# Value and output weights of a local attention folded into one matrix per head, in a six-layer stack on one core

## The chip, the cores and the metric

The program runs on one core of one Trainium2 chip. The metric is the device time of one execution in microseconds (us), the median of several runs.

## What is computed

The input x has 8 batches of 512 tokens with 128 features. Two blocks follow each other, each behind a layer norm that is scaled and shifted per batch, and each is added to x with a gate. The first block is a causal attention with 16 heads of 8. The second is a stack of 6 layers; each is a windowed attention with 16 heads of 64 followed by a gated feed-forward part, both on x with its upper 64 features shifted by one token:

```python
def attn_layer(x, Wqkv, qs, ksc, Wo):
    q, k, v = jnp.split(x @ Wqkv, 3, -1)          # each 1024 wide: 16 heads of 64
    q = l2norm(q) * qs; k = l2norm(k) * ksc       # then rotary tables on both
    out = local_attention(q, k, v)                # windows of 32, each sees itself and the one before
    return out.reshape(b, n, INNER) @ Wo          # 1024 -> 128

for i in range(6):
    x = attn_layer(shift_tokens(x), Wqkv[i], q_scale[i], k_scale[i], Wo[i]) + x
    x = ffn_layer(shift_tokens(x), ln_g[i], ln_b[i], W1[i], b1[i], W2[i], b2[i]) + x
```

All of it is float32. A head's part of the result is softmax(q k) times v_h times Wo_h, where v_h = x Wv_h is 64 wide and Wo_h takes 64 to 128.

## The kernel before

There are three stages, one after the other: `modulated_attention` (names `at_`), `local_stack` (names `st_`), and a short `last_residual` (`lr_`). Every engine has its own hand-written program, with loops that are unrolled by hand at both ends, and semaphores between the engines.

**The first attention** goes through the batches, with 16 steps to a batch, one head a step. Its TensorE order is a table, `M_JOBS`: (step, part, kind, batch offset, index). These products go in turn into two PSUM banks, and each waits until the one two places before has been taken out. Beside them, in batches 1 to 6, this stage prepares one layer of the stack per batch: the SP queue loads a third of Wqkv (`split_weights`, the q, k or v part, 128x1024), GpSimd splits it at L1516 and L1518 into a rounded part and a remainder (two fp32r numbers in place of one float32), and SP stores both in a DRAM scratch, `wqkv_parts`. The rotary tables are made in the same batches.

**The stack** has 6 layers times 8 batches, so 48 units, and a unit is four steps, one for each tile of 128 tokens: 192 steps in all. A step works on four tiles at once, in a software pipeline. For the new tile it makes q, k and v (L455): for each, 6 fp32r products of 128x512, three per half of the width. For the tile one back it transposes the rotated q and k (`tq`, `tk`, L472) and multiplies them (`sim`, L485: for each of 8 head pairs and 4 windows a product that has 32 output rows). For the tile two back it transposes the weights (`pt`, L477) and multiplies them with v (`o`, L497: again 8 times 4 products with 32 output rows). For the tile three back it transposes o (`ot`, L505) and multiplies with Wo (`z`, L465), which gives the layer's result with features on the partitions. Once a unit come the products of the feed-forward part of earlier units: `m1` in step 3, `m2` in step 0, `h` in step 1 and `y` in step 2. The order of TensorE is the list in `jobs_of`; `slot_free` makes each product wait until the last user of its PSUM banks has been read out.

The others, for each step:

- VectorE sums the squares of q (L710), multiplies it with the cosines (L714) and the sines (L728, two halves), then the same for k; L721 puts a floor under the sums. Then come mask (L749), maximum (L753), the sum of the weights and its reciprocal (L757, L760), the addition of z to x (L784), and the division of o by the sums (L792).
- GpSimd adds the cosine and sine parts of q and of k (L826 twice), makes one Newton step for the norms (four small operations, L833 to L839), multiplies q and k with them (L846 twice), and subtracts the maximum from the scores of the tile one back (L874). In step 1 it does five operations of the feed-forward norm first (L853 to L861).
- ScalarE squares q and k, copies the transposed tiles out of PSUM, copies v to `v_tok`, and takes the exponentials.
- The SP queue builds `v_bd`, the values of each window with those of the window before, by ten DMAs a step from `v_tok` (`spread_v`, L371 to L379; eight in step 0): 64 partitions x 2 KB each for three of four windows, 32 partitions for the rest. It waits for the `o` product that still reads the half of `v_bd` it writes.

At the last unit of a layer SP loads the next layer's `wqkv` (three DMAs of 1 MB, L337), as soon as the last tile's q, k and v have been made.

## Time and profile before

| | |
|---|---|
| time, median of 3 runs | 3995.38 us (3992.62 to 4001.01) |
| the profiled execution: its own time | 4002.27 us |
| its span, first to last instruction | 4000.5 us |
| mean granted TensorE clock in it | 0.985 of full speed |
| TensorE busy (PE) | 3733.8 us, 93% |
| its weight loads (PEld) | 2927.6 us, 73% |
| VectorE busy (DVE) | 3151.4 us, 79% |
| ScalarE busy (ACT) | 2570.7 us, 64% |
| GpSimd busy (POOL) | 2781.7 us, 70% |

Busy is the time in which at least one instruction of an engine runs. PE and PEld run beside each other. A row of a list of groups gives the source line, the engine, the operation, what is written and what is read, the number of instructions, and then the busy time and the mean of one; matmuls overlap in the array, so their mean is longer than the busy time divided by their number. A row of a timeline has the start in us from the beginning of the span, the length in us, the instruction, and how many were merged. DMA share is how busy the 16 DMA engines were on average.

### The profile page before, as it was taken

What the parts mean: (1) busy time and instruction counts of PE and PEld (TensorE: products, weight loads), DVE (VectorE), ACT (ScalarE), POOL (GpSimd) and SP (SyncE); (2) the same over time, 40 slices, a digit from 0 to 9 for tenths busy, and PEclk for the clock granted to TensorE, in tenths of its full rate; (3) what the DMA queues carried; (4) which work ended last, traced back from release to release, by engine and by line L of the source; (5) the groups of instructions that cost most, each with busy time, mean ns of one, the idle gap of its engine ahead of it and who ended that gap; (6) DMA issues with size and microseconds to landing.
All of it is one profiled execution on the core that took longest, in us unless ns stands there. A gap on an engine that the chain in (4) does not pass through costs nothing. (4 is left out here: it accounts for less than half of the span.)

```text
span 4000.5 us, 109740 instructions
## 1 busy us (share of the span) xinstructions
PE 3733.8 (93%) x42284; PEld 2927.6 (73%) x42284; DVE 3151.4 (79%) x4328; ACT 2570.7 (64%) x3589; POOL 2781.7 (70%) x2249
## 2 busy tenths in 40 slices
PE   6998897799999999999999999999999999999996
PEld 4766675677777777777777777777777777777774
DVE  4666664888888888888888888888888888888884
ACT  3555554566666666666666666666666767676763
POOL 2554552777777777777777777777777777777772
PEclk9999998999999999999999999999999999999998
DMA  1122110322223222232222232222322223222222
GB/s 42 59 74 73 66 68 13 100 66 60 62 63 100 66 58 64 55 103 63 68 53 66 82 79 64 61 61 62 102 66 62 60 60 99 62 70 54 68 54 62
DMA packets 157178, 267.01 MB, mean 67 GB/s; under 512 B 32062, under 2 KB 51644, under 8 KB 152380
## 3 DMA queue, kind: packets, MB, share of 16 engines
q1 hardware_dynamic: 157116, 266.19, 24.7%
q8 instruction: 38, 0.62, 0.1%
q14 instruction: 24, 0.20, 0.0%
HBM read 44.81 MB, written 26.21 MB: 18 GB/s over the span
## 5 line engine op out<-in xcount | busy, mean ns | idle before, releaser
L826 POOL TENSOR_TENSOR st_qk_rot<-st_qk_rot,st_qk_sq 128x1024 f32<-128x1024 f32 x384 | 920.5, 2402 | 692.7 <-DVE st_qk_sq L728 692.7
L455 PE MATMUL st_ps<-st_wqkv,st_xs 128*128 128x512 f32 x3456 | 949.6, 410 | 25.8 <-issue 18.3
L455 PEld LDWEIGHTS st_ps<-st_wqkv,st_xs 128*128 128x128 f32 x3456 | 608.2, 189 | 194.6 <-issue 75.2
L846 POOL TENSOR_TENSOR st_qk_rot<-st_qk_rot,st_rn 128x1024 f32<-128x1024 f32 x384 | 723.1, 1904 | 15.0
L710 DVE TENSOR_REDUCE st_nt<-st_qk_sq 128x16 f32<-128x1024 f32 x384 | 466.2, 1214 | 234.6 <-ACT st_qk_sq L573 233.2
L728 DVE TENSOR_TENSOR st_qk_sq<-st_ps,st_rot 128x512 f32<-128x512 f32 x768 | 490.1, 678 | 0.0
L714 DVE TENSOR_TENSOR st_qk_rot<-st_ps,st_rot 128x1024 f32<-128x1024 f32 x384 | 466.1, 1214 | 9.8 <-PE st_ps L472 9.8
L472 PE MATMUL st_ps<-consts_sb,st_qk_rot 128*128 128x128 f32 x3072 | 402.2, 274 | 27.9 <-DVE st_hid L802 14.9
L571 ACT ACTIVATE st_qk_sq<-st_ps 128x512 f32<-128x512 f32 x192 | 115.0, 599 | 486.3 <-PE st_ps L455 485.8
L472 PEld LDWEIGHTS st_ps<-consts_sb,st_qk_rot 128*128 128x128 f32 x3072 | 355.8, 141 | 94.1 <-DVE st_hid L802 34.7
L465 PEld LDWEIGHTS st_ps<-st_oT,st_wo 128*128 128x128 f32 x3072 | 368.8, 192 | 69.5 <-issue 67.7
L1458 DVE TENSOR_REDUCE at_nmx<-at_s 128x1 f32<-128x512 f32 (+3 forms) x512 | 236.9, 486 | 209.3 <-PE at_s L1103 208.5
L608 ACT ACTIVATE st_k_bd<-st_ps 64x1024 f32<-64x1024 f32 x384 | 389.5, 1014 | 3.1 <-PE st_ps L472 0.8
L485 PE MATMUL st_ps<-st_k_bd,st_qT 128*32 128x128 f32 x12288 | 375.2, 274 | 3.0 <-ACT st_k_bd L608 3.0
L465 PE MATMUL st_ps<-st_oT,st_wo 128*128 128x128 f32 x3072 | 376.2, 276 | 0.5 <-ACT st_oT L632 0.3
L497 PE MATMUL st_ps<-st_v_bd,st_probT 128*32 128x128 f32 x12288 | 375.2, 274 | 1.3 <-ACT st_probT L640 1.3
L874 POOL TENSOR_TENSOR st_s<-st_s,st_mx 128x1024 f32<-128x1024 f32 x192 | 366.0, 1906 | 6.1 <-DVE st_mx L753 6.1
L1279 ACT ACTIVATE at_probT<-at_t 128x512 f32<-128x512 f32 (+1 forms) x384 | 201.3, 526 | 255.8 <-PE at_t L1122 248.1
L485 PEld LDWEIGHTS st_ps<-st_k_bd,st_qT 128*32 128x32 f32 x12288 | 326.4, 110 | 35.6 <-ACT st_k_bd L608 20.5
L497 PEld LDWEIGHTS st_ps<-st_v_bd,st_probT 128*32 128x32 f32 x12288 | 323.7, 110 | 24.5 <-issue 1.5
L522 PE MATMUL st_ps<-st_xc,st_w 128*128 128x512 f32 (+1 forms) x576 | 261.8, 604 | 52.6 <-DVE xT_sb L784 43.2
L1542 POOL TENSOR_TENSOR at_qs<-at_q,consts_sb 128x512 fp32r<-128x512 f32 x128 | 135.3, 1074 | 216.8 <-DVE at_q L1409 200.0
(144 smaller groups left out, 6944.8 us busy)
## 6 DMA issues: line engine op xcount, KB each, us to landing
st_v_bd<-st_v_tok SPq DMA_DIRECT2D x1152, 128.0 KB, 2.4
st_v_bd<-st_v_tok SPq DMA_DIRECT2D x672, 64.0 KB, 2.1
wqkv_parts<-at_w_parts SPq DMA_DIRECT2D x18, 1024.0 KB, 4.6
st_wqkv<-wqkv_parts SPq DMA_DIRECT2D x18, 1024.0 KB, 7.0
at_w_raw<-in_wqkv SPq DMA_DIRECT2D x18, 512.0 KB, 5.1
rotary_tables<-at_rot SPq DMA_DIRECT2D x6, 512.0 KB, 3.4
st_rot<-rotary_tables SPq DMA_DIRECT2D x24, 128.0 KB, 2.4
st_wo<-in_wo SPq DMA_DIRECT2D x6, 512.0 KB, 4.4
```

Source lines behind the costliest of these rows:

```text
L455: last = pe.matmul(out[:, c * 512:(c + 1) * 512], xs[:, x_part, t * P:(t + 1) * P], rhs, start=(n == 0), stop=(n == len(PASSES) - 1))
L465: last = pe.matmul(out[:, 0:P], wo[:, c, :], oT[:, c * P:(c + 1) * P], start=(c == 0), stop=(c == IC - 1))
L472: last = pe.transpose(out[:, c * P:(c + 1) * P], src[:, c * P:(c + 1) * P], ident)
L485: last = pe.matmul(out[g * WIN:(g + 1) * WIN, c * P:(c + 1) * P], qT[:, par, c * P + g * WIN:c * P + (g + 1) * WIN], k_bd[:, c, :, key:key ...
L497: last = pe.matmul(out[g * WIN:(g + 1) * WIN, c * P:(c + 1) * P], probT[:, c * P + g * WIN:c * P + (g + 1) * WIN], v_bd[:, par, g, :, c * ...
L608: last = act.activation(k_bd[rows, :, a, WIN + t1 * P:WIN + (t1 + 1) * P], src[rows, :, :], ACT.Copy)
L710: dve.tensor_reduce(nt[:, 2 + par, heads], qk_sq[:, cols].rearrange("p (h d) -> p h d", d=DH), AX.X, ALU.add).then_inc(ss_sum, 1)
L714: dve.tensor_tensor(qk_rot[:, cols].rearrange("p (h d) -> p h d", d=DH), slot_of("qk"[a], 0, t).rearrange("p (h d) -> p h d", d=DH), rot[: ...
L728: last = dve.tensor_tensor(dst[:, :, g, :], src[:, :, 1 - g, :], sines.unsqueeze(1).to_broadcast([P, HEADS, DH // 2]), ALU.mult)
L826: pool.tensor_tensor(qk_rot[:, cols], qk_rot[:, cols], qk_sq[:, cols], ALU.add).then_inc(rot_done[a], 1)
L846: pool.tensor_tensor(view, view, rn[:, par, heads_of(a)].unsqueeze(2).to_broadcast([P, HEADS, DH]), ALU.mult).then_inc(normed[a], 1)
L874: pool.tensor_tensor(scores, scores, mx[:, tt % 2, :].unsqueeze(2).to_broadcast([P, HEADS, 2 * WIN]), ALU.subtract).then_inc(shifted, 1)
```

## The change

The product of the value weights and the output weights of each head, Wv_h Wo_h (128x128), is computed once a layer in the first attention. In the stack v is then x times that, 128 wide a head and 2048 for all 16 heads, in two halves `v0` and `v1` (even and odd heads). The weights times these values are summed over the head pairs directly in PSUM: the `z` product now has the form of the old `o` product, and its 128x128 result, tokens on the partitions, is copied and transposed once (`zt`). `ot` and the product with `wo` are gone. The division by the sums moves from VectorE after `o` to GpSimd before the weights are transposed (`scaled`), so that `pt` and everything after it work on a tile three back. `v_tok` and `v_win` (formerly `v_bd`) hold twice the bytes. The last 32 rows of a tile's values, which the next tile needs, are first copied by DMA into `v_held`. Several banks, and the order of the work on ScalarE and VectorE in a step, are different.

```diff
-H_BANKS = ((0, 1), (6, 7), (2, 3))
+H_BANKS = ((6, 7), (0, 1), (4, 5))
+PROJ = ("q", "k", "v0", "v1")
...
             return [tile("q", 0, 0, 1), tile("tq", 1, 2, 3), tile("k", 0, 4, 5), tile("tk", 1, 6, 7),
-                    tile("v", 0, 2, 3), tile("ot", 3, 0, 1), tile("sim", 1, 6, 7), tile("pt", 2, 2, 3), *feed,
-                    tile("z", 3, 0), tile("o", 2, 4, 5), *hidden]
+                    tile("v0", 0, 2, 3), tile("pt", 3, 0, 1), tile("sim", 1, 6, 7), tile("v1", 0, 0, 1), tile("z", 3, 2),
+                    *feed, *hidden, tile("zt", 3, 7)]
...
+                    for kind in ("v0", "v1"):
+                        sp.wait_ge(taken[kind], tiles_done(u, 0, t))
+                    if t < TILES - 1:
+                        d, carried = ((-1, 3), (-1, 2), (0, 1))[t]
+                        if alive(u, d):
+                            sp.wait_ge(carry_in[carried % 2], carry_count(u, d, carried))
+                        for a in range(2):
+                            sp.dma_start(v_held[held_rows(t, a), :], v_tok[P - WIN:P, par, a, :]).then_inc(held_in[par], 16)
+                    sp.wait_ge(ready["z"], tiles_done(u, 0, t))
...
-                        if what == "wqkv" and t == TILES - 1:
+                        if what == "wqkv" and t >= TILES - 2:
-                            for kind in "qkv":
-                                sp.wait_ge(ready[kind], tiles_done(u, 0, t))
+                            for kind in (("q", "k"), ("v0", "v1"))[t - (TILES - 2)]:
+                                sp.wait_ge(ready[kind], tiles_done(u, 0, TILES - 1))
                                 load_wqkv(layer + 1, kind)
                         spread_v(u, t)
...
+                            elif kind == "z":
                                 pe.wait_ge(taken["pt"], tiles_done(u, d, index))
-                                pe.wait_ge(vbd_in[par], spread_count(u, d, index))
+                                pe.wait_ge(win_in[par], spread_count(u, d, index))
...
                                 for c in range(IC):
                                     for g in range(WPT):
                                         last = pe.matmul(
-                                            out[g * WIN:(g + 1) * WIN, c * P:(c + 1) * P],
+                                            out[g * WIN:(g + 1) * WIN, 0:P],
                                             probT[:, c * P + g * WIN:c * P + (g + 1) * WIN],
-                                            v_bd[:, par, g, :, c * DH:(c + 1) * DH], start=True, stop=True)
+                                            v_win[:, par, g, c * P:(c + 1) * P], start=(c == 0), stop=(c == IC - 1))
...
+                        def copy_v(a):
+                            act.wait_ge(ready[f"v{a}"], n)
+                            if not (start and n < 3):
+                                act.wait_ge(win_in[t % 2], spread_count(u, d2, t2))
+                                if t2 < TILES - 1:
+                                    act.wait_ge(held_in[t2 % 2], held_count(u, d2, t2))
+                            act.activation(v_tok[:, t % 2, a, :], slot_of(f"v{a}", 0, t), ACT.Copy).then_inc(taken[f"v{a}"], 1)
...
-                            dve.tensor_tensor(
-                                o[:, :].rearrange("p (h d) -> p h d", h=HEADS),
-                                slot_of("o", d2, t2).rearrange("p (h d) -> p h d", h=HEADS),
-                                den[:, t2 % 2, 1, :].unsqueeze(2).to_broadcast([P, HEADS, DH]),
-                                ALU.mult).then_inc(taken["o"], 1)
...
+                        d, tt = divmod(t - 2, TILES)
+                        if alive(u, d):
+                            pool.wait_ge(den_ready, 2 * (n - 2))
+                            weights = s[:, tt % 2, :].rearrange("p (h k) -> p h k", h=HEADS)
+                            pool.tensor_tensor(weights, weights, den[:, tt % 2, 1, :].unsqueeze(2).to_broadcast([P, HEADS, 2 * WIN]),
+                                               ALU.mult).then_inc(scaled, 1)
...
-SPLIT_STEPS = (2, 6, 14)
+SPLIT_STEPS = (5, 11)
...
+                    elif kind == "fold":
+                        rows, half = slice(g // 2 * DH, (g // 2 + 1) * DH), g % 2
+                        pe.wait_ge(taken["vt"], count(b, 0, 2, half))
+                        pe.wait_ge(fold_in, (b - 1) * 16 + 16)
+                        for i in range(TILES):
+                            c = TILES * half + i
+                            last = pe.matmul(out[:, i * P:(i + 1) * P], wvT[rows, c, :], wo_l[rows, c, :],
+                                             start=True, stop=True)
```

In `M_JOBS` of the first attention two jobs `vt` (four transposes of the raw value weights each, steps 2 and 3) and four jobs `fold` (four products each, two in step 7, one each in steps 11 and 14) are added for each layer. ScalarE copies both out of PSUM, and VectorE subtracts to get the remainder of each `fold`. GpSimd splits only the q and k parts now. Four parts of 1 MB a layer are stored and loaded, not three.

TensorE's program in the stack, the last step of the second unit (names: `st_s` weights, `st_wqkv` projection weights, `xT_sb` is x). Before:

```order
L455 MATMUL st_ps<-st_wqkv,st_xs 128x512 x6
L472 MATMUL st_ps<-consts_sb,st_qk_rot 128x128 x8
L455 MATMUL st_ps<-st_wqkv,st_xs 128x512 x6
L472 MATMUL st_ps<-consts_sb,st_qk_rot 128x128 x8
L455 MATMUL st_ps<-st_wqkv,st_xs 128x512 x6
L505 MATMUL st_ps<-consts_sb,st_o 128x128 x8
L485 MATMUL st_ps<-st_k_bd,st_qT 32x128 x32
L477 MATMUL st_ps<-consts_sb,st_s 128x128 x8
L509 MATMUL st_ps<-xT_sb,consts_sb 128x512
L465 MATMUL st_ps<-st_oT,st_wo 128x128 x8
L497 MATMUL st_ps<-st_v_bd,st_probT 32x128 x32
```

The same step in the changed kernel:

```order
L460 MATMUL st_ps<-st_wqkv,st_xs 128x512 x6
L475 MATMUL st_ps<-consts_sb,st_qk_rot 128x128 x8
L460 MATMUL st_ps<-st_wqkv,st_xs 128x512 x6
L475 MATMUL st_ps<-consts_sb,st_qk_rot 128x128 x8
L460 MATMUL st_ps<-st_wqkv,st_xs 128x512 x6
L480 MATMUL st_ps<-consts_sb,st_s 128x128 x8
L488 MATMUL st_ps<-st_k_bd,st_qT 32x128 x32
L460 MATMUL st_ps<-st_wqkv,st_xs 128x512 x6
L500 MATMUL st_ps<-st_v_win,st_probT 32x128 x32
L507 MATMUL st_ps<-xT_sb,consts_sb 128x512
L469 MATMUL st_ps<-consts_sb,st_z_tok 128x128
```

A fourth group of six projections has come in; the eight transposes of o and the eight products with `wo` are gone; one transpose stands at the end, behind the feed-forward product.

GpSimd's program in a step of the stack, in the changed kernel:

```order
L830 TENSOR_TENSOR st_qk_rot<-st_qk_rot,st_qk_sq 128x1024 [waits st_rot_read_q]
L830 TENSOR_TENSOR st_qk_rot<-st_qk_rot,st_qk_sq 128x1024 [waits st_rot_read_k]
L837 TENSOR_TENSOR st_nt<-st_rn 128x32 [waits st_rn_ready]
L839 TENSOR_TENSOR st_nt<-st_nt,st_ss 128x32 [waits st_pool_own]
L841 TENSOR_TENSOR st_nt<-consts_sb,st_nt 128x32 [waits st_pool_own]
L843 TENSOR_TENSOR st_rn<-st_rn,st_nt 128x32 [waits st_pool_own]
L850 TENSOR_TENSOR st_qk_rot<-st_qk_rot,st_rn 128x1024 [waits st_rot_done_q,st_rn_final]
L850 TENSOR_TENSOR st_qk_rot<-st_qk_rot,st_rn 128x1024 [waits st_rot_done_k,st_rn_final]
L878 TENSOR_TENSOR st_s<-st_s,st_den 128x1024 [waits st_den_ready]
L885 TENSOR_TENSOR st_s<-st_s,st_mx 128x1024 [waits st_max_ready]
```

Before, the ninth of these rows (L878) did not exist; the others are the same.

The SP queue at the last unit of a layer, in the changed kernel, from the last but one tile on:

```order
L349 DMA st_wqkv<-wqkv_parts 128x2048 [waits st_q_ready]
L349 DMA st_wqkv<-wqkv_parts 128x2048 [waits st_k_ready]
L382 DMA st_v_held<-st_v_tok 32x1024 [waits st_v0_taken,st_v1_taken,st_carry_in1]
L382 DMA st_v_held<-st_v_tok 32x1024
L389 DMA st_v_win<-st_v_held 32x1024 [waits st_z_ready,st_held_in1]
L389 DMA st_v_win<-st_v_held 32x1024
L394 DMA st_v_win<-st_v_tok 64x1024 x3
L396 DMA st_v_win<-st_v_tok 32x1024
L394 DMA st_v_win<-st_v_tok 64x1024 x3
L396 DMA st_v_win<-st_v_tok 32x1024
L349 DMA st_wqkv<-wqkv_parts 128x2048 [waits st_v0_ready]
L349 DMA st_wqkv<-wqkv_parts 128x2048 [waits st_v1_ready]
```

Before, the three loads of `st_wqkv` stood together, ahead of the last tile's ten DMAs. Now the loads for `v0` and `v1` stand behind ten DMAs that wait for a `z` product. (One load of a rotary table, which stands ahead of the last two rows and another ahead of the first two, is not shown.)

## Rows read from the trace of the kernel before

**Rows 1.** Stretches: PE, PEld, DVE, ACT, POOL busy, clock, DMA share, GB/s
```profile
420.00:500.00 80.00, 71.95 (x533) 54.16 (x533) 52.46 (x108) 46.46 (x90) 44.88 (x40) 1.00 0.20 72
725.00:3948.00 3223.00, 3116.62 (x38250) 2469.24 (x38249) 2699.70 (x3436) 2188.36 (x2860) 2447.53 (x1955) 1.00 0.26 68
```
**Rows 2.** Timeline of TensorE in one step of the stack
```profile
1225.88 1.67 PE L455 MATMUL st_ps<-st_wqkv,st_xs 128*128 128x512 f32 x6
1227.38 1.04 PE L472 MATMUL st_ps<-consts_sb,st_qk_rot 128*128 128x128 f32 x8
...
1232.12 1.06 PE L505 MATMUL st_ps<-consts_sb,st_o 128*128 128x128 f32 x8
1233.11 1.96 PE L485 MATMUL st_ps<-st_k_bd,st_qT 128*32 128x128 f32 x64
...
1237.04 1.95 PE L465 MATMUL st_ps<-st_oT,st_wo 128*128 128x128 f32 x16
1238.92 1.96 PE L497 MATMUL st_ps<-st_v_bd,st_probT 128*32 128x128 f32 x64
1240.80 1.66 PE L455 MATMUL st_ps<-st_wqkv,st_xs 128*128 128x512 f32 x6
```
**Rows 3.** Timeline of TensorE: first projection of step 1, step 2, next step 1
```profile
1509.60 1.66 PE L455 MATMUL st_ps<-st_wqkv,st_xs 128*128 128x512 f32 x6
...
1529.59 1.65 PE L455 MATMUL st_ps<-st_wqkv,st_xs 128*128 128x512 f32 x6
...
1576.82 1.65 PE L455 MATMUL st_ps<-st_wqkv,st_xs 128*128 128x512 f32 x6
```
**Rows 4.** Groups of GpSimd from 800 to 3800 us
```profile
L826 POOL TENSOR_TENSOR st_qk_rot<-st_qk_rot,st_qk_sq 128x1024 f32<-128x1024 f32 x358 | 858.5, 2404 | 641.5 <-DVE st_qk_sq L728 641.5
...
L874 POOL TENSOR_TENSOR st_s<-st_s,st_mx 128x1024 f32<-128x1024 f32 x179 | 341.2, 1906 | 0.0
```
**Rows 5.** Timeline of GpSimd: the feed-forward norm of step 1, then a step 2
```profile
1513.91 1.04 POOL L853 TENSOR_TENSOR st_xc<-st_rstd 128x512 f32<-128x512 f32 x1
...
1517.40 1.29 POOL L859 TENSOR_TENSOR st_xc<-st_xc,st_rstd 128x512 f32<-128x512 f32 x1
...
1520.01 4.69 POOL L826 TENSOR_TENSOR st_qk_rot<-st_qk_rot,st_qk_sq 128x1024 f32<-128x1024 f32 x2
...
1536.68 2.38 POOL L826 TENSOR_TENSOR st_qk_rot<-st_qk_rot,st_qk_sq 128x1024 f32<-128x1024 f32 x1 [5.09 <-DVE st_qk_sq L728]
1540.37 2.48 POOL L826 TENSOR_TENSOR st_qk_rot<-st_qk_rot,st_qk_sq 128x1024 f32<-128x1024 f32 x1 [1.31 <-DVE st_qk_sq L728]
1542.81 0.23 POOL L833 TENSOR_TENSOR st_nt<-st_rn 128x32 f32<-128x32 f32 x1
...
1544.11 3.77 POOL L846 TENSOR_TENSOR st_qk_rot<-st_qk_rot,st_rn 128x1024 f32<-128x1024 f32 x2
```
**Rows 6.** Timeline of VectorE in the same two steps
```profile
1517.65 1.07 DVE L721 TENSOR_SCALAR st_ss<-st_nt 128x32 f32<-128x32 f32 x1
...
1538.78 0.32 DVE L721 TENSOR_SCALAR st_ss<-st_nt 128x32 f32<-128x32 f32 x1
```
**Rows 7.** Timeline of the SP queue at a layer change
```profile
1217.97 1.41 SPq L337 DMA_DIRECT2D st_wqkv<-wqkv_parts  x3
1225.89 1.17 SPq L371 DMA_DIRECT2D st_v_bd<-st_v_tok  x2
...
1231.58 0.59 SPq L379 DMA_DIRECT2D st_v_bd<-st_v_tok  x1
```
**Rows 8.** Stretch in that layer change, columns as in Rows 1
```profile
1225.00:1227.00 2.00, 1.90 (x36) 1.46 (x26) 1.59 (x3) 0.73 (x2) 2.00 (x2) 1.00 1.01 430
```
**Rows 9.** The page: DMA issues, KB each, us from issue to landing
```profile
st_v_bd<-st_v_tok SPq DMA_DIRECT2D x672, 64.0 KB, 2.1
```
**Rows 10.** ScalarE from 800 to 3800 us: copies of v to v_tok
```profile
L618 ACT ACTIVATE st_v_tok<-st_ps 128x1024 f32<-128x1024 f32 x179 | 183.7, 1027 | 4.3
```
**Rows 11.** First attention: products with 32 output rows that add up over key tiles
```profile
L1148 PE MATMUL at_m<-at_probT,at_v_pad 128*32 128x512 f32 x256 | 35.0, 619 | 5.2 <-DVE at_k L1409 4.8 <-ACT at_probT L1279 0.4
```

More of the change, by code:

```diff
@@ L232, in local_stack @@
         nt = sb("nt", [P, 4, 2 * HEADS])
-        v_tok = sb("v_tok", [P, 2, INNER])
-        v_bd = sb("v_bd", [P, 2, WPT, 2, INNER // 2])
+        v_tok = sb("v_tok", [P, 2, 2, INNER])
+        v_win = sb("v_win", [P, 2, WPT, INNER])
+        v_held = sb("v_held", [P, INNER])
         qT = sb("qT", [P, 2, INNER])
@@ L240, in local_stack @@
         probT = sb("probT", [P, INNER])
[L241 to L242 removed]
+        z_tok = sb("z_tok", [P, P])
         xc = sb("xc", [P, N])
@@ L382, in unit @@
+                        sp.dma_start(v_win[a * 2 * WIN + WIN:(a + 1) * 2 * WIN, par, 0, :], v_tok[0:WIN, par, a, :])\
+                          .then_inc(win_in[par], 16)
                 def unit(u, layer=None, what=None):
                     for t in range(TILES):
-                        if what == "wo" and t == 2:
-                            sp.wait_ge(ready["z"], tiles_done(u, -1, TILES - 1))
-                            sp.wait_ge(small_in, 64)
-                            load_wo(layer)
@@ L406, in layer_loads @@
                     u0 = layer * BATCH
-                    unit(u0, layer, None if first else "wo")
+                    unit(u0, layer)
                     unit(u0 + 1, layer, None if first else "w12")
@@ L459, in unit @@
                                         last.then_inc(q_half, 1)
-                            elif kind == "z":
-                                pe.wait_ge(taken["ot"], tiles_done(u, d, index))
-                                pe.wait_ge(wo_in, layer_of(u, d) * 16 + 16)
-                                for c in range(IC):
-                                    last = pe.matmul(out[:, 0:P], wo[:, c, :], oT[:, c * P:(c + 1) * P],
-                                                     start=(c == 0), stop=(c == IC - 1))
+                            elif kind == "zt":
+                                pe.wait_ge(taken["z"], tiles_done(u, d, index))
+                                last = pe.transpose(out[:, 0:P], z_tok[:, :], ident)
                             elif kind in ("tq", "tk"):
@@ L767, in unit @@
                                               ALU.subtract).then_inc(taken["m1"], 1)
+                        if alive(u, d1):
+                            dve.wait_ge(taken["sim"], n - 1)
+                            dve.tensor_reduce(mx[:, t1 % 2, :], scores, AX.X, ALU.max).then_inc(max_ready, 1)
+                        if t == 2 and alive(u, 1):
+                            remainder_half(u, 1, 0)
+                        if t == 1 and alive(u, -2):
+                            gate(2)
+                        d3, t3 = divmod(t - 3, TILES)
+                        if alive(u, d3):
+                            dve.wait_ge(ready["zt"], n - 3)
+                            for rows, first in ((LOW, 0), (HIGH, 1)):
+                                x = columns_of(batch_of(u, d3), t3 * P + first, P, rows)
+                                last = dve.tensor_tensor(x, slot_of("zt", d3, t3)[rows, 0:P], x, ALU.add)
+                            last.then_inc(taken["zt"], 1)
+                        if t == 0 and alive(u, 0) and alive(u, -1):
+                            remainder_half(u, 0, 1)
                         if t == 2 and alive(u, -2):
@@ L1074, in _ @@
             def _(pe):
+                for kind in ("vt", "fold"):
+                    pe.sem_inc(ready[kind], PER[kind])
+                    pe.sem_inc(taken[kind], PER[kind])
+                pe.sem_inc(fold_high, PER["fold"])
                 pe.wait_ge(w_in, 80)
```

262 lines of the change are left out of this document (138 added, 124 removed), and 4 rows, old and new, of the table M_JOBS.

## The prediction

> **What bounds the kernel now.** I read the page's busy times first, where TensorE leads with 93% (the table above). Then the table of stretches: in the stack, from 725 to 3948 us, TensorE is busy 3116.6 of 3223 us (97%), at a granted clock of 1.00, the level of 2.4 GHz, with VectorE at 84%, GpSimd at 76% and the DMA engines at 26%; in the first attention it is 71.95 of 80 us (90%) [rows 1]. So both stages are bound by TensorE's own work, and in the stack hardly anything waits for another engine. The timeline gives the size: a unit of four steps is 1576.82 - 1509.60 = 67.2 us, of which step 1, with the large feed-forward product, takes 20.0 us [rows 3], and a plain step (step 0) 1240.80 - 1225.88 = 14.9 us [rows 2]. What matters next is who has room. GpSimd waited 641.5 us for VectorE before L826 [rows 4], in a stretch of 179 steps: 3.6 us of a step.
>
> **TensorE's work in a step.** The start of one group to the start of the next is what a group costs; all from [rows 2].
> - Gone: eight transposes `ot`, 1233.11 - 1232.12 = 0.99 us; eight products with Wo, 1238.92 - 1237.04 = 1.88 us.
> - Added: six projections, 1227.38 - 1225.88 = 1.50 us; one transpose `zt`, an eighth of 0.99, 0.12 us. `zt` waits for ScalarE's copy of z, but a feed-forward product stands between them in each step (`m1` in the listing above), and it is longer than a 128x128 copy.
> - `o` becomes `z` with the same 32 products, 1240.80 - 1238.92 = 1.88 us: nothing.
>
> Together -1.25 us, times 192 steps: **-240 us**. The time saved is real only as long as nobody else is late.
>
> **GpSimd.** Each step gets one operation more, a 128x1024 product with a broadcast operand, the shape of L874: 1.91 us [rows 4]. Its work in a step was 2 x 2.40 (L826) + 1.30 (the Newton step for the norms, 1544.11 - 1542.81) + 3.77 (L846 twice) + 1.91 = 11.8 us [rows 4, 5], and the feed-forward norm adds 1520.01 - 1513.91 = 6.1 us once a unit [rows 5]: 53 us of 67.2. It becomes 4 x 13.7 + 6.1 = 60.9 us, against TensorE's 67.2 - 5.0 = 62.2. So GpSimd goes to 98% of the new period, and the two drive each other: `tq` needs L846, L826 needs the products that VectorE makes once `tq` has read the old tile. The slack that is left, 1.3 us a unit, is as large as one wait of GpSimd between its two L826, 1.31 us [rows 5]. That wait has a cause: L721, a small operation of VectorE, lies across the first L826. It starts at 1538.78 and ends with it (1536.68 + 2.38 = 1539.06), and only then come k's sines, 1.3 us. At 1517.65 it started 0.25 us after L859 and took 1.07 us, to the end of that one [rows 5, 6]. So VectorE waits in L721 for a running GpSimd operation.
> The Trainium skill (page "SBUF — State Buffer", section "Who interferes with whom") says that `tensor_scalar` on VectorE can take the port pair that it shares with GpSimd, and that whoever comes first holds it for the whole instruction. By that rule the trace agrees, with 1.07 us for a 128x32 operation; taken alone, it would put the upper bound below, +125 us, in place of my +38.
> I choose 0.8 us a unit of lost time, a bit over half of one such wait, as TensorE and GpSimd are late in turns: 48 x 0.8 = **+38 us**. Bounds: 0 (60.9 fits into 62.2), and three such waits in a unit (none in step 1, where the feed-forward norm makes GpSimd late anyhow): 60.9 + 3.9 = 64.8, which is 2.6 us over 62.2, +125 us.
>
> **VectorE and ScalarE.** VectorE loses the 128x1024 division, ScalarE trades the copy of o for one of v1 and a small one of z. VectorE was at 84% and gets lighter [rows 1]: nothing for both. Since `pt` now works three tiles back, the new chain sum, division on GpSimd, transpose has a whole step of time: it costs latency, once.
>
> **The DMAs for the windows.** The same ten DMAs a step carry twice the bytes (2.1 MB), and two more go to `v_held`, for which nobody waits. Issue is one each 0.63 us (1225.89 to 1231.58 for nine) and a small one lands 2.1 us after it [rows 7, 9]: 7.8 us from the first issue to the last landing. Issue does not go with bytes: 1 MB loads are issued in 1.41 us for three [rows 7]. The engines moved 68 GB/s at a share of 0.26 [rows 1], so 262 GB/s at most with 2 KB rows, and 430 with 8 KB rows [rows 8]: 2.1 MB take 4.9 to 8.0 us, so D, the whole, is 7.8 to 10 us. What closes a loop is: z done, D, the copy of v0 to `v_tok` (1.03 us [rows 10]), z again (1.88 us, it uses a bank of v0), 0.3 us of handovers. D + 3.2 is 11.0 to 13.2 us, and the plain step is 14.9 - 1.25 = 13.7. Hidden, but with as little as 0.5 us to spare at the upper end. Taken as nothing.
>
> **Layer changes, five.** Before, the three loads stood ahead of the last tile's ten DMAs and had landed when the next unit began (issued at 1217.97, engines full until 1227 [rows 7, 8]). Now v0 and v1 come behind ten DMAs that wait for the `z` of the last step, which ends some 12.5 us into it (13.7 less `m1` and `zt`): with 6.3 us of issue and a rotary table they are issued at about 19.5, and 1 MB at 430 GB/s with 2.1 us to land makes 24. TensorE wants v0 in the next step at 13.7 + 4.7 = 18.4 (1232.12 - 1225.88 - 1.50 = 4.7 for what stands ahead of v [rows 2]). That is 5.6 us of standing still, of which the slack takes back some: 5 x 5 = **+25 us**. Bounds 0 and 9 us each (both loads): 0 to +45.
>
> **First attention, six layers.** Added for each are eight transposes (0.99) and 16 float32 products of 128 columns (1.88 for eight, so 3.76): 4.75 us of TensorE, in a stage where it is busy 90% [rows 1, 2]. GpSimd loses one split of three, which frees nobody. Six times 4.75, and some waits for the copies of `fold`, as two of these follow each other: **+30 us**. Bounds: 10 (the idle tenth takes most) and 50 (each of the four `fold` jobs makes TensorE wait for two copies, about 0.9 us). The stack's first loads are 4 MB and not 3, at 430 GB/s: **+2 us**.
>
> **Sum.** -240 + 38 + 25 + 30 + 2 = -145. The profiled execution took 4002.3 us, 6.9 above the median of 3995.4, so 3857 for it and **3850 us** as a median. A difference of 0.2%, 8 us, is what can be told from no change here.
>
> **The rivals.**
> 1. *GpSimd sets the pace* (0.19). Each plain step keeps the 1.31 us wait, since GpSimd is now nearly always in L826 when L721 comes: a unit of 64.8 us, -240 + 125 + 57 = -58: 3937 us. For it: both rows of L721, and 98% load. Against it: when GpSimd is late by more than that, L721 meets an earlier operation and the wait is hidden, as at 1520.01, where the two L826 run in 4.69 us without a gap [rows 5]. The page's rule named above leads to this rival.
> 2. *Everything fits* (0.22). GpSimd's slack is enough, the layer loads are not missed, the first attention absorbs half: -240 + 5 + 12 + 2, about 3775 us. For it: TensorE at 97% shows how well this order hides waits [rows 1].
> 3. *The window DMAs close the loop, and it is slower* (0.08). If the ten issues took time with their bytes, 1.26 us each, D would be 1.26 x 9 + 2.1 and something for the queue, 14 us. A plain step would be 17.2 us, a unit 3 x 17.2 + 19 = 70.6: 48 x 3.4 + 57 = +220: 4215 us. It decides from D = 12.5 us on, where a unit is 66.0 and the 57 us of the other terms tip it. Against it: issue times of 64 KB and 1 MB are alike [rows 7].
> 4. *The products that now add up in one place lose their overlap* (0.03). The 32-row products run four at a time, 1.88 us for 32 [rows 2]; `z` now adds eight times into the same columns. Were they to run one by one, this is 5.6 us a step more, nearly 5000 us. Against it: L1148 adds up in the same way, with 32 output rows, at 35.0 / 256 = 0.137 us for 512 columns [rows 11], the rate of the products here (1.88 / 64 = 0.029 for 128).
>
> **Chances.** The forecast 0.46, with its own range of 3815 to 3900; rivals 0.19, 0.22, 0.08, 0.03; 0.02 for no visible change, by several bounds at once. Faster by over 0.2%: 0.87; within: 0.02; slower: 0.11. The range that leaves out the two slow cases and a little at both ends is 3765 to 3945.
>
> **What would show it.** A unit (from one first projection of step 1 to the next) of 62 to 64 us; TensorE at 96% or more of the stack and GpSimd at 95%; waits before L830 down from 641 us to under 150; a wait of TensorE of some 5 us at v0 in the first step of a layer, five times; the first attention longer by 25 to 35 us. It is wrong if ScalarE's copies of v wait for DMAs (D too long), or if TensorE waits for L850 in every step.

## The result, and the profile after

| | before | after |
|---|---|---|
| median of 4 runs each | 3997.92 us | 4049.28 us (4040.14 to 4062.88) |
| ratio, 95% interval | | 1.013 (1.010 to 1.017) |
| the profiled execution, its span | 4002.3, 4000.5 us | 4053.2, 4051.4 us |

The kernel became 1.3% slower; 3.7% faster was forecast. The page of the kernel after, busy times:

```profile
PE 3593.3 (89%) x39260; PEld 2654.6 (66%) x39260; DVE 3040.5 (75%) x4160; ACT 2606.9 (64%) x3817; POOL 3112.2 (77%) x2430
```
TensorE is busy 140 us less, and the program takes 51 us more. The columns of the stretches are those of [rows 1]; the first line is its counterpart, the others lie at the first layer change, where loads from DRAM run beside the window DMAs:

```profile
725.00:3948.00 3223.00, 2920.23 (x34566) 2156.66 (x34566) 2587.58 (x3239) 2193.86 (x3038) 2805.26 (x2143) 0.98 0.65 141
1264.00:1266.00 2.00, 2.00 (x26) 1.28 (x18) 2.00 (x3) 1.63 (x3) 1.01 (x1) 1.00 0.95 389
1266.00:1278.00 12.00, 8.12 (x95) 5.79 (x87) 10.16 (x14) 7.43 (x11) 11.69 (x10) 1.00 1.04 255
1278.00:1290.00 12.00, 3.92 (x14) 3.22 (x14) 1.69 (x3) 0.00 (x0) 2.80 (x2) 0.57 0.75 227
```
TensorE fell from 97% to 91% of the stack: 303 us in which it does nothing, where it was 106. The DMA share rose from 0.26 to 0.65. Who waits, from 900 to 3800 us (total, times, longest), in two parts of the list:

```profile
POOL st_qk_rot L830 <- DVE st_qk_sq L736: 230.4, 215, 3.7
ACT st_v_tok L598 <- DMA st_v_win<-st_v_tok: 229.7, 125, 2.9
...
DVE st_den L766 <- ACT st_s L632: 149.4, 125, 2.6
```
The second line did not exist before: ScalarE stands 1.8 us on average, 125 times, in front of a copy of v, until the window DMAs of the tile that had this half of `v_tok` have landed. The page on the DMA issues (KB each, us from issue to landing) says why; [rows 9] had 2.1:

```profile
st_v_win<-st_v_tok SPq DMA_DIRECT2D x1152, 256.0 KB, 4.6
st_v_win<-st_v_tok SPq DMA_DIRECT2D x384, 128.0 KB, 4.8
...
st_wqkv<-wqkv_parts SPq DMA_DIRECT2D x24, 1024.0 KB, 7.8
```
And the timelines of three engines in one step, first the SP queue:

```profile
1493.44 1.17 SPq L389 DMA_DIRECT2D st_v_win<-st_v_held  x2
1494.65 1.96 SPq L394 DMA_DIRECT2D st_v_win<-st_v_tok  x3
1496.65 1.10 SPq L396 DMA_DIRECT2D st_v_win<-st_v_tok  x1
1497.79 2.82 SPq L394 DMA_DIRECT2D st_v_win<-st_v_tok  x3
1500.66 0.79 SPq L396 DMA_DIRECT2D st_v_win<-st_v_tok  x1
```
```profile
1505.64 1.02 ACT L598 ACTIVATE st_v_tok<-st_ps 128x1024 f32<-128x1024 f32 x1 [2.16 <-DMA st_v_win<-st_v_tok]
```
```profile
1506.79 1.95 PE L500 MATMUL st_ps<-st_v_win,st_probT 128*32 128x128 f32 x64 [0.91 <-ACT st_v_tok L598]
```
The last DMA is issued at 1500.66 and lands 4.9 us later, at 1505.56; ScalarE copies at 1505.64, and TensorE has stood still for 0.91 us when `z` may start. Over all steps from 900 to 3800 us the median from the first issue of these ten to the last landing is 12.1 us; before it was 7.8. While only DMAs between parts of SBUF run, the DMA engines are full at 219 GB/s (columns of [rows 1]):

```profile
1496.00:1505.00 9.00, 8.09 (x102) 6.71 (x101) 7.60 (x10) 6.16 (x8) 8.84 (x7) 1.00 1.03 219
```
The layer change, SP queue and TensorE:

```profile
1274.88 0.99 SPq L396 DMA_DIRECT2D st_v_win<-st_v_tok  x1
1275.92 1.25 SPq L367 DMA_DIRECT2D st_rot<-rotary_tables  x1
1277.21 0.94 SPq L349 DMA_DIRECT2D st_wqkv<-wqkv_parts  x2
```
```profile
1272.56 1.64 PE L460 MATMUL st_ps<-st_wqkv,st_xs 128*128 128x512 f32 x6 [0.79 <-DMA st_wqkv<-wqkv_parts]
...
1286.09 2.90 PE L460 MATMUL st_ps<-st_wqkv,st_xs 128*128 128x512 f32 x6 [11.02 <-DMA st_wqkv<-wqkv_parts]
```
The load of v0 is issued at 1277.21 behind the windows and has landed at 1285.95; the six projections behind the pause take 2.90 us and not 1.64, with the clock at 0.57 in that stretch.

**Where the time went.** I measure units from one `m1` product to the next. Before, each is 67.2 us (at the very start and end 67.3 and 66.4), over layer changes too. After, 41 plain ones take 65.5 to 65.9 (the first 67.5 and the last 65.0), and the five over a layer change 78.4, 75.8, 81.3, 76.5 and 76.3. A batch of the first attention (from one `wo` product to the next) goes from 78.2 to 85.2 us and more. Against the forecast of 3857 for the profiled execution, 196 us are missing:

| term | forecast | measured | lost |
|---|---|---|---|
| 41 plain units | 63.0 us (67.2 - 5.0 + 0.8) | 65.7 | 111 |
| 5 over a layer change | 63.0 + 5 = 68 | 77.7 | 48 |
| first weight load | 696.8 + 30 | 744.5 | 18 |
| from there to the first `m1` | 121.0 + 2 | 127.4 | 4 |
| behind the last whole unit (draining, last stage) | | | 15, the rest |

The third row has scatter of its own. The first attention is the same program in the kernel after and in kernels 1 to 10 below, and its first weight load comes between 736.7 and 749.1 us in these eleven traces, with a mean clock of 0.97 to 0.99 from 200 to 700 us.

### The profile page after: what moved, and what is told of

It is laid out like the page before. It is cut to its first block and busy times, and to the rows that moved or that the text cites. A ratio compares the mean times of both kernels' runs of the same rounds, so it can differ in the third digit from the quotient of the medians.

```text
span 4051.4 us, 104528 instructions
## 1 busy us (share of the span) xinstructions
PE 3593.3 (89%) x39260; PEld 2654.6 (66%) x39260; DVE 3040.5 (75%) x4160; ACT 2606.9 (64%) x3817; POOL 3112.2 (77%) x2430
## 5 line engine op out<-in xcount | busy, mean ns | idle before, releaser
L460 PE MATMUL st_ps<-st_wqkv,st_xs 128*128 128x512 f32 x4608 | 1272.6, 412 | 95.8 <-DMA st_wqkv<-wqkv_parts 52.7
L830 POOL TENSOR_TENSOR st_qk_rot<-st_qk_rot,st_qk_sq 128x1024 f32<-128x1024 f32 x384 | 912.1, 2380 | 276.1 <-DVE st_qk_sq L736 276.0
L460 PEld LDWEIGHTS st_ps<-st_wqkv,st_xs 128*128 128x128 f32 x4608 | 815.0, 190 | 332.7 <-issue 189.6
L850 POOL TENSOR_TENSOR st_qk_rot<-st_qk_rot,st_rn 128x1024 f32<-128x1024 f32 x384 | 739.5, 1947 | 15.0
L598 ACT ACTIVATE st_v_tok<-st_ps 128x1024 f32<-128x1024 f32 x384 | 391.1, 1019 | 269.2 <-DMA st_v_win<-st_v_tok 253.2
L500 PE MATMUL st_ps<-st_v_win,st_probT 128*32 128x128 f32 x12288 | 376.5, 275 | 99.2 <-ACT st_v_tok L598 95.5
L500 PEld LDWEIGHTS st_ps<-st_v_win,st_probT 128*32 128x32 f32 x12288 | 325.3, 110 | 174.3 <-issue 165.7
L878 POOL TENSOR_TENSOR st_s<-st_s,st_den 128x1024 f32<-128x1024 f32 x192 | 366.5, 1909 | 4.4 <-DVE st_den L769 4.4
L766 DVE TENSOR_REDUCE st_den<-st_s 128x16 f32<-128x1024 f32 x192 | 233.3, 1215 | 164.3 <-ACT st_s L632 164.3
L625 ACT ACTIVATE st_probT<-st_ps 128x1024 f32<-128x1024 f32 x192 | 197.0, 1026 | 216.0 <-PE st_ps L480 215.9
```

The source lines that it names most:

```text
L460: last = pe.matmul(out[:, c * 512:(c + 1) * 512], xs[:, x_part, t * P:(t + 1) * P], wqkv[:, PROJ.index(kind), w_part, c * 512:(c + 1) * 51 ...
L500: last = pe.matmul(out[g * WIN:(g + 1) * WIN, 0:P], probT[:, c * P + g * WIN:c * P + (g + 1) * WIN], v_win[:, par, g, c * P:(c + 1) * P], ...
L598: act.activation(v_tok[:, t % 2, a, :], slot_of(f"v{a}", 0, t), ACT.Copy).then_inc(taken[f"v{a}"], 1)
L830: pool.tensor_tensor(qk_rot[:, cols], qk_rot[:, cols], qk_sq[:, cols], ALU.add).then_inc(rot_done[a], 1)
L850: pool.tensor_tensor(view, view, rn[:, par, heads_of(a)].unsqueeze(2).to_broadcast([P, HEADS, DH]), ALU.mult).then_inc(normed[a], 1)
L878: pool.tensor_tensor(weights, weights, den[:, tt % 2, 1, :].unsqueeze(2).to_broadcast([P, HEADS, 2 * WIN]), ALU.mult).then_inc(scaled, 1)
```

## The experiments

Kernel 9 was run five times, each of the other ten once. The kernel before took 3996.3 us beside kernels 1, 2, 3 and 7, 3993.0 beside 4, 5, 6 and 8, and 4000.0 beside the last three. The changed kernel's own four runs lie between 4040 and 4063 us, so a single time that differs by less than some 20 us tells little; the units, which repeat within 0.3 us in a trace, tell more. Theory A was that the window DMAs set the unit through ScalarE's copies; its rival that GpSimd does.

**1. Half the bytes.** Each window DMA moves half of its columns; the others keep zeros, so that half of v never reaches `z`. One of the four kinds of DMA, all cut alike:

```diff
-sp.dma_start(v_win[rows, par, g, :], v_tok[(g - 1) * WIN:(g + 1) * WIN, par, a, :])
+sp.dma_start(v_win[rows, par, g, 0:INNER // 2], v_tok[(g - 1) * WIN:(g + 1) * WIN, par, a, 0:INNER // 2])
```


> The changed kernel, but every DMA from v_tok, to v_held and to v_win moves only the first 512 of its 1024 columns (the values behind the rest stay zero, so the weighted sums leave out half of the head pairs); counts, waits and all other work are the same. Theory A, the window DMAs close the loop (last landing, copy of v0, z): a unit falls from 65.7 us to 62.5 to 63.5, ScalarE's waits for DMA before the copies of v (230 us from 900 to 3800) vanish, and the layer changes shrink by a few us each since the engines are free sooner. Theory B, GpSimd sets the pace: a unit stays at 65 to 66 us. In both the first attention stays at 85 us a batch. Time by A about 3900 us, by B about 4030.

Measured: 4015.2 us. A DMA of 128 KB lands after 2.4 us and ScalarE no longer waits for one, but the units are 65.3, some 67.0; layer changes 70.6 to 72.1. Theory A missed: with its wait gone, another stood almost as high, once a unit before the large feed-forward product (it is explained under 3):

```profile
st_v_win<-st_v_tok SPq DMA_DIRECT2D x1152, 128.0 KB, 2.4
```
```profile
PE st_ps L520 <- ACT st_xc L639: 77.6, 38, 2.1
```

**2. No division on GpSimd.** The product of weights and reciprocal sums is left out (z is then not normalised).

```diff
-pool.wait_ge(den_ready, 2 * (n - 2))
-pool.tensor_tensor(weights, weights, den[:, tt % 2, 1, :].unsqueeze(2).to_broadcast(...), ALU.mult).then_inc(scaled, 1)
-pe.wait_ge(scaled, tiles_done(u, d, index))
+pe.wait_ge(exp_ready, tiles_done(u, d, index))
```


> The changed kernel without GpSimd's product of the weights with the reciprocal sums (so the weights are not divided); pt waits for the exponentials instead. Theory A (DMAs close the loop): GpSimd had slack, a unit stays within 0.5 us of 65.7 us and the time at 4030 to 4050 us. Theory B (GpSimd sets the pace): 4 x 1.9 us less work, a unit falls to 62.5 to 63.5 us and the time to about 3920 us.

Measured: 4045.3 us, units 65.7. GpSimd has 1.91 us a step less to do and simply waits longer:

```profile
POOL st_qk_rot L830 <- DVE st_qk_sq L736: 481.0, 260, 3.6
ACT st_v_tok L598 <- DMA st_v_win<-st_v_tok: 225.9, 124, 2.4
```
So GpSimd alone isn't the limit either.

**3. A semaphore for each half of `v_tok`.** v0's copy waits for the four window DMAs that read v0, not for all eight that read `v_tok`.

```diff
-.then_inc(win_in[par], 16)
+.then_inc(win_in[par][a], 16)
...
-act.wait_ge(win_in[t % 2], spread_count(u, d2, t2))
+act.wait_ge(win_in[t % 2][a], spread_count(u, d2, t2))
```


> The changed kernel with one semaphore for each half of v_tok: the copy of v0 waits only for the DMAs that read v0's half, the copy of v1 for those of v1's. Same work, same bytes. Theory A (the copy of v0 waits for the last landing of all ten DMAs): the first half has landed some 3 us earlier, a unit falls from 65.7 us to 63 to 63.5, and ScalarE's DMA waits fall from 230 us to under 40; time about 3930 us. Theory B (GpSimd sets the pace): a unit stays at 65 to 66 us, the wait only changes its name.

Measured: 4047.2 us, units 65.3 and some 67.0, and no wait of ScalarE for a DMA. What had been behind it shows in GpSimd, ScalarE and TensorE of step 1:

```profile
1498.11 1.91 POOL L886 TENSOR_TENSOR st_s<-st_s,st_mx 128x1024 f32<-128x1024 f32 x1
...
1504.81 1.26 POOL L866 TENSOR_TENSOR st_xc<-st_xc 128x512 f32<-128x512 f32 x1
```
```profile
1506.28 0.81 ACT L640 ACTIVATE st_xc<-st_xc,st_ln_b,st_ln_g 128x512 f32<-128x512 f32 x1 [3.04 <-POOL st_xc L866]
```
```profile
1507.39 1.98 PE L521 MATMUL st_ps<-st_xc,st_w 128*128 128x512 f32 x4 [2.02 <-ACT st_xc L640]
```
GpSimd does the feed-forward norm behind the division and the subtraction of the maxima; it ends at 1506.1, so the large product waits 2 us. In the units of 67.0 the clock also falls after that pause (0.74 and 0.84 in the two stretches of 4 us from 1572), and the product takes 7.1 us and not 5.4. Each of the eleven units of 67.0 has one stretch of 3.4 us at the lower level, and none of those of 65.3 has one.

**4. Both together.** Experiments 2 and 3 in one.

> Both walls taken away at once: one semaphore for each half of v_tok, and GpSimd's product of the weights with the reciprocal sums left out. Alone, each left the unit at 65.3 to 67.0 and at 65.7 us. Theory C (two limits of nearly the same height: the window DMAs, and GpSimd, whose late feed-forward norm holds up the large product h): the unit falls to 62.3 to 63.5 us and the wait of TensorE for ScalarE's st_xc (2.0 us a unit) is gone; time about 3920 us. Rival D (some other wait, of TensorE for VectorE or of the order of the products): the unit stays above 64.5 us.

Measured: 3938.4 us, units of 63.2 throughout. Alone, kernel 2 came out 4 us and kernel 3 2 us below 4049, both within the scatter, with units of 65.7 and of 65.3 and 67.0; together they give 111. Two limits of almost the same height: that is theory C, and it holds.

**5. The feed-forward norm first.** Kernel 3, and GpSimd's norm at the end of step 0, ahead of the maxima, with ScalarE's use of it ahead of the exponentials.

```diff
-if t == 1 and alive(u, -2):
+if t == 0 and alive(u, -2):
...
-act.activation(s[:, t2 % 2, :], s[:, t2 % 2, :], ACT.Exp).then_inc(exp_ready, 1)
...
 act.activation(xc[:, :], xc[:, :], ACT.Identity, bias=column(ln_b, P, layer_of(u, -2)),
                scale=column(ln_g, P, layer_of(u, -2))).then_inc(ff_xn, 1)
+act.activation(s[:, t2 % 2, :], s[:, t2 % 2, :], ACT.Exp).then_inc(exp_ready, 1)
```


> One semaphore for each half of v_tok, as before; and GpSimd does the five operations of the feed-forward norm at the end of step 0, ahead of its subtraction of the maximum, not at the start of step 1; ScalarE applies the norm's gain (st_xc) before its exponentials in step 1. Same work, GpSimd's division kept. Theory C: h no longer waits for st_xc (2.0 us), the clock does not fall after that gap, and the unit is 63 to 63.8 us in place of 65.3 and 67.0; time about 3960 us. Rival E (GpSimd's total work is the limit, wherever the norm stands): the unit stays at 65 us or more.

Measured: 3996.3 us (before, on that chip, 3993.0), units 64.6, between the two readings: less gained than expected. Nothing is left out here, and 53 us are back.

**6. Window DMAs in turns over the partition halves.**

```diff
-for a in range(2):
-    for g in range(1, WPT):
+for g in range(1, WPT):
+    for a in range(2):
...
+for a in range(2):
```
(The last loop is now around the two smaller DMAs.)


> The changed kernel with the eight window DMAs of a step issued in turn for partitions 0 to 63 and 64 to 127, instead of four for the one half and then four for the other. Theory P (a transfer over 64 partitions reaches only a part of what the DMA engines can do, so that turns help): landing of the 256 KB ones falls from 4.6 to under 3.5 us, ScalarE's DMA waits from 230 us to under 80. Rival (SBUF to SBUF costs what it costs by bytes): landings and waits stay within 10% and the unit at 65.7 us.

Measured: 4021.5 us, units 65.3. The landings stay at 4.8 and 4.6 us, so that part missed; ScalarE's wait for DMAs fell from 230 to 150 us all the same. The landings of each burst show a path: the last of the ten lands 4.1 us after its issue and no longer 5.1 (medians), and from the first issue to the last landing it is 11.5 us, not 12.1.

**7. All weight loads ahead of the windows.** The four loads of the next layer stand ahead of the last-but-one tile's windows.

```diff
-if what == "wqkv" and t >= TILES - 2:
+if what == "wqkv" and t == TILES - 2:
-for kind in (("q", "k"), ("v0", "v1"))[t - (TILES - 2)]:
+for kind in PROJ:
```


> The changed kernel with all four loads of the next layer's projection weights ahead of the tenth-last tile's DMAs, that is before the window DMAs of the last but one tile's step, as near as possible to where they stood before the change. Theory: the 12 us that each of five layer changes costs over a plain unit (an interval of 75.8 to 81.4 us against 65.7) come from v0's load standing behind ten DMAs. They should fall to 4 us or less each, and the clock should not drop there: 40 to 50 us less, about 4003 us. Rival: the DMA engines are full anyway, 2 MB more ahead of the windows only delays these, and the interval stays above 73 us.

Measured: 4035.8 us, layer changes 73.3 to 75.4, above the 70 expected. The stall moved; its longest is now ScalarE's:

```profile
ACT st_v_tok L598 <- DMA st_v_win<-st_v_tok: 273.1, 129, 10.2
```
Four megabytes ahead of the windows make the windows late.

**8. Loads in the middle.** Kernel 3, with q, k and v0 ahead of those windows and v1 between their halves.

```diff
+next_weights("q", "k", "v0")
+spread_v(u, t, (lambda: next_weights("v1")) if changes else None)
```


> One semaphore for each half of v_tok, as before; and at a layer change the loads for q, k and v0 stand ahead of the last but one tile's window DMAs, v1's load between its two halves. Theory: v0's weights are there when asked for, and the copy of v0 waits for only half of the windows: a layer change costs at most 5 us over a unit (10 to 12 before, 9 with all four loads ahead), so the intervals are 70 to 72 us. Rival: 4 MB of loads and 2.1 MB of windows in one step fill the engines whatever the order, and it stays at 74 us.

Measured: 4022.6 us, layer changes 68.3, 69.9, 73.1, 68.9 and 68.3: 3 to 8 us over a unit, where they were 10 to 16.

**9. The cures together** (3, 5 and 8), timed against before.

> The three cures together: a semaphore for each half of v_tok, GpSimd's feed-forward norm at the end of step 0, and the next layer's weights for q, k and v0 loaded ahead of the last-but-one tile's window DMAs with v1 between its halves. The parts measured 64.6 us a unit (half waits and norm first) and layer changes 3 to 5 us longer than a unit (loads in the middle). If they add: units 64.6, the five intervals over a layer change 67 to 71 instead of 74.6 to 77.3, 30 to 40 us below the run with norm first (3996), so 3955 to 3970, about 1% faster than before. If the loads' traffic meets the earlier norm in a new wait: units stay 64.6 but layer changes 72 or more, 3980 or more.

Measured: 3965.1 us (3962.9 to 3974.6, 5 runs), before 4000.0; ratio 0.992 (0.990 to 0.993). The parts add up as expected: units 64.6; layer changes 70.0, 72.8, 73.4, 68.1 and 69.6. It computes all of the reference and is faster than both kernels. What remains is in GpSimd's waits, its timeline and VectorE's, and the stretch from 900 to 3800 us:

```profile
POOL st_qk_rot L835 <- DVE st_qk_sq L741: 204.0, 182, 2.2
```
```profile
1504.32 2.39 POOL L835 TENSOR_TENSOR st_qk_rot<-st_qk_rot,st_qk_sq 128x1024 f32<-128x1024 f32 x1
1508.02 2.39 POOL L835 TENSOR_TENSOR st_qk_rot<-st_qk_rot,st_qk_sq 128x1024 f32<-128x1024 f32 x1 [1.31 <-DVE st_qk_sq L741]
```
```profile
1506.06 0.69 DVE L734 TENSOR_SCALAR st_ss<-st_nt 128x32 f32<-128x32 f32 x1
1506.66 1.28 DVE L741 TENSOR_TENSOR st_qk_sq<-st_ps,st_rot 128x512 f32<-128x512 f32 x2
```
```profile
900.00:3800.00 2900.00, 2732.23 (x32404) 2001.50 (x32397) 2394.77 (x3020) 2072.38 (x2843) 2611.37 (x2001) 1.00 0.67 145
```
182 waits of 1.1 us in 179 steps: the wait of 1.31 us of [rows 5], now in an engine with little to spare. GpSimd is busy 2611 us and waits 204 us for VectorE here, 97% of 2900 together.

**10. The same without the division.**

> As the kernel with all three cures, with GpSimd's multiplication of the weights by their reciprocal sums left out. If DMAs waited for and GpSimd's pace are all that stood between the forecast unit and the measured one: units of 62.5 to 63.2 us (the forecast's saving of 4.2 from 67.2 gives 63.0), layer changes 66 to 70, 3890 to 3910. If another wall stands near (ScalarE's exponentials, VectorE's maxima): units 64 or more, 3940 or more.

Measured: 3903.4 us, units 63.2, layer changes 70.8, 70.2, 69.9, 67.3 and 68.2. From 1500 to 1750 us TensorE is busy as it was before the change (columns of [rows 1]), and a step 0 shows its price:

```profile
1500.00:1750.00 250.00, 241.02 (x2906) 177.77 (x2905) 211.96 (x270) 182.60 (x255) 204.77 (x164) 1.00 0.66 141
```
```profile
1508.61 1.65 PE L464 MATMUL st_ps<-st_wqkv,st_xs 128*128 128x512 f32 x6
...
1519.59 1.95 PE L505 MATMUL st_ps<-st_v_win,st_probT 128*32 128x128 f32 x64
1521.47 1.12 PE L517 MATMUL st_ps<-st_xc,consts_sb 128*128 128x512 f32 x2
1522.44 0.27 PE L473 MATMUL st_ps<-consts_sb,st_z_tok 128*128 128x128 f32 x1
1522.46 1.64 PE L464 MATMUL st_ps<-st_wqkv,st_xs 128*128 128x512 f32 x6
```
96% busy, and a plain step of 1522.46 - 1508.61 = 13.85 us, where 13.7 was forecast.

**11. A quarter of the new products.** The changed kernel, with one in four of the first attention's new transposes and products; its last projections are thus made of one block repeated.

```diff
-for i in range(TILES):
+for i in range(1):
     c = TILES * half + i
```


> The changed kernel with only one in four of TensorE's transposes of Wv and of its products Wv Wo (ScalarE and VectorE copy the one block four times over, so their work is the same size; the last projections use the wrong product). TensorE's added work a batch in the first attention falls from 5.25 us to 1.3. If that work is the price: a batch 85.2 -> 80.5 to 81.5, the first weight load 22 to 28 us earlier, in all 4020 to 4030. If the price lies in waits that the new jobs make in ScalarE's and VectorE's order (both shared PSUM banks held): a batch 83.5 or more, 4040 or more.

Measured: 4062.1 us, the first load at 754.1 and not 744.5, outside the scatter of 736.7 to 749.1. By its numbers this is the second reading, but not by its reason: TensorE is idle for 8.8 to 10.4 us of a full batch, where it was 9.4 to 9.8. The batches start at 85.8 us and grow to 92.1 with less work in them. In the kernel after, TensorE's wait before one product of the projections looks the same in two batches, and only behind one of them is the work slow (timeline, then the stretches around it, columns of [rows 1]):

```profile
357.70 1.12 PE L1213 MATMUL at_m<-at_hT,at_wqk 128*128 128x512 f32 x2 [1.51 <-DVE at_q L1479]
...
442.91 1.97 PE L1213 MATMUL at_m<-at_hT,at_wqk 128*128 128x512 f32 x2 [1.52 <-DVE at_q L1479]
```
```profile
357.00:361.00 4.00, 3.30 (x19) 2.54 (x19) 2.34 (x5) 1.40 (x3) 3.84 (x5) 1.00 0.00 0
443.00:447.00 4.00, 4.00 (x14) 2.78 (x14) 1.54 (x4) 0.96 (x2) 3.92 (x4) 0.57 0.00 0
```
In kernel 11 the same place:

```profile
445.00:449.00 4.00, 4.00 (x10) 2.53 (x11) 1.48 (x4) 0.96 (x2) 3.92 (x4) 0.51 0.00 0
449.00:453.00 4.00, 4.00 (x19) 2.74 (x22) 2.70 (x5) 2.29 (x4) 1.96 (x4) 0.50 0.00 0
453.00:457.00 4.00, 4.00 (x37) 2.15 (x30) 0.73 (x2) 0.62 (x2) 0.69 (x1) 0.71 0.87 263
```
The granted clock sits at its lower level, 1.2 GHz, for about 10 us and not 4. From 200 to 700 us it averages 0.92 there and 0.98 in the kernel after. The batch of 92.1 us has a mean clock of 0.89, so it would take about 92.1 x 0.89 = 82.0 at full clock, an estimate that shortens its waits too and comes near what the work left out would give (85.2 - 3.9 = 81.3). In this one run the work was saved and its time given back in clock.

## Why the prediction was wrong

**TensorE's work: right.** -1.25 us a step held: 13.85 us against 13.7, once nobody else was late (run 10). The 32 products of `z` take 1521.47 - 1519.59 = 1.88 us, as those of `o` did; rival 4 is out.

**The window DMAs: the step that failed.** "D, the whole, is 7.8 to 10 us", "Taken as nothing". In the timeline above, D is 1505.56 - 1493.44 = 12.1 us, which is also the median. Two terms were under-sized. The ten issues, the two from `v_held` among them, take 1500.66 - 1493.44 = 7.2 us from first to last, where I had 5.7; that the time doesn't go with bytes I had argued from three loads issued one behind another. And I let the last one land 2.1 us after its issue, a figure of transfers with half the bytes, where it needs 4.9. By my own loop D + 3.2 is then 15.3 us against a step of 13.7. I had set a bandwidth bound (8.0 us, at 262 GB/s) beside the issue time, without a landing behind it: 2.1 MB at the measured 219 GB/s are 9.6 us, and with the 2.3 us in which the first one landed 11.9, an estimate close to D. The landing time is that of the backlog: of the same 128 KB, the two at the head of the burst land after 2.3 us and the one at its end after 4.9. Rival 3 had this loop, but it looked for all of the extra time in the issues. Its place of decision, D = 12.5, was nearly met, but it charged 17.2 us to a step, and the unit came to 65.7 and not 70.6. My condition "ScalarE's copies of v wait for DMAs" is what the list of waits shows. Where the semaphore goes was a second thing I didn't weigh: one for all eight window DMAs from `v_tok` made v0's copy wait for v1's readers, and run 3 took that wait away with the same work and the same bytes.

**GpSimd: it costs time, as forecast, but more, and for a wait whose cause I misread.** The forecast was +0.8 us a unit. With the DMA wait gone (runs 5 and 9) a unit is 64.6, without the division 63.2: 1.4 us a unit for the division. A unit of 64.6 is that of rival 1 (64.8), with its wait of 1.31 us in each step. I argued that such waits hide behind an engine that is late; 182 of them did not. But the cause that I gave for it, VectorE's L721 held up by the running GpSimd operation, is a small part of it in [rows 5, 6]:

```profile
L721 DVE TENSOR_SCALAR st_ss<-st_nt x192: 172/332/1107, 715.6 to 3905.8; 128x32 f32<-128x32 f32 x192
```
```profile
1539.02 1.27 DVE L728 TENSOR_TENSOR st_qk_sq<-st_ps,st_rot 128x512 f32<-128x512 f32 x2
```
The shortest L721 takes 0.17 us (ns, least, median and most in the first line) and this one took 0.32, so the collision cost 0.15 us of the 1.31. The rest is VectorE's own work: k's sines take 1.27 us and begin behind L721. In run 9 the same operation (L734) took 0.69 us. No run takes the collision away, so what it costs in a unit stays open.

I also named the feed-forward norm only as 6.1 us of load. Where it stood mattered more: behind the division, its result reached TensorE 2 us late (run 3), and moving it, with nothing left out, was worth 51 us between runs 3 and 5 (53 us from the first to the last `m1` of their traces).
The expectation "waits before L830 under 150 us" also missed, 230 us, since GpSimd was held up along with the rest.
L721's wait for GpSimd, real at 1517.65 in [rows 6] (1.07 us), has a larger relative. In the group of VectorE's that makes `xs`, which reads two operands from SBUF, 128x256 took 408 ns before and 1403 after:

```profile
L694 DVE TENSOR_TENSOR st_xs<-xT_sb,st_xs 128x256 fp32r<-128x256 f32 x86 | 120.6, 1403 | 9.2 <-ACT st_xs L548 7.9
```
By the rule of the Trainium skill (page "SBUF — State Buffer", section "Who interferes with whom"), a VectorE instruction with two SBUF inputs contends with a GpSimd instruction that reads SBUF, since its second input comes through the read interface that they share. The trace agrees: from 900 to 3800 us all of them began while GpSimd was idle before and took 0.41 us; after, all 86 begin within a product of L850, and the median one ends 0.28 us behind it. In kernel 3 one takes 2.11 us from 1527.23, just behind the start of two GpSimd products at 1527.15. What counts is where they stand and not how busy GpSimd is: in run 2 it is busy 77% of that stretch, as before (76%), and they take 1.42 us. No run tried what this costs.

**Two limits at once.** The sum priced the DMAs and GpSimd one by one, against TensorE alone. Each measured as next to nothing when removed by itself (65.7 to 65.3 and 67.0 in turns, and 65.7 to 65.7), and 2.5 us a unit when both went: 63.2, where my terms without GpSimd's say 62.2; the last 1.0 us stays open.

**Layer changes: right place, 5 us each forecast, 14.7 measured** (77.7 against 63.0). I had v0 issued 7.0 us after the end of `z` (19.5 less 12.5) and landed 4.5 us after that, at 430 GB/s. It was issued 9.5 us after it, as the ten issues ahead take longer, and landed 8.7 us later (1285.95; 6.5 to 10.8 in the five layer changes): the last window DMA ahead of it, issued at 1274.88, landed itself only at 1283.33. Then came a clock of 0.57. Other placings of the loads brought the excess down to 3 to 9 us (runs 8 and 9).

**First attention: +48, forecast +30, bounds 10 to 50.** The new groups cost 5.2 us a batch from their starts to the next ones', where I had 4.75. TensorE's busy time in a batch also rises by 5.2, from 70.25 (237.13 to 315.36) to 75.47 us (248.36 to 333.56), but at different clocks, 0.98 and 1.00: before, one stretch of 3.4 us ran at the lower level with TensorE busy in all of it. At one clock the rise is nearer 6.9 us, an estimate, and I can't name the other 1.7. The idle tenth took nothing. It grew by 1.8 us a batch, most of it a wait of `den` for the `fold` jobs' bank (1.3 us):

```profile
405.77 1.05 PE L1203 MATMUL at_m<-consts_sb,at_aT 128*128 128x4 f32 x8 [1.32 <-DVE at_fold_parts L1502]
```
More comes from the clock in the later batches (88.4 us at 0.96, 89.6 at 0.94), and up to 12 us of the 48 can be the scatter between traces of the same program. What makes the clock fall behind one pause of 1.5 us and not behind another like it stays open; run 11, a single execution, shows only that less work between the pauses didn't shorten a batch.

## What to carry over

When a change loads several engines that were idle a fifth of the time, compare each with the new period and then with one another: a cure for one of two equal limits measures as nothing, and it takes a run without both to see either. Price a burst of DMAs from its first issue to the landing of its last one, at the size that it will have, count what is in the queue ahead of it, and give each consumer a semaphore for what it needs and no more. An engine that comes near its limit should do first what the busiest engine waits for.
